# Edge loop of a graph network on one core: the running sums carried on VectorE instead of TensorE, and three copies and comparisons in another order

## The reference, cut to what matters

```python
source = x[src]; target = x[dst]
h = jax.nn.relu(concatenate([source, target, edge_attr]) @ W_msg1 + b_msg1)
aggregated = segment_sum(h @ W_msg2 + b_msg2, dst)        # layer 0
agg = segment_sum(x[src] + edge_attr_16 @ ew.T + eb, dst)  # layer 1
```

## Time and profile before

| | us |
|---|---|
| median of 3 runs | 4364.23 (4362.29 to 4392.64) |
| the profiled execution | 4381.03 |
| its span | 4379.2 |
| first gather to last store of the edge loop | about 130 to 1586 |
| GpSimd busy in that stretch | 1169.59 |
| TensorE busy in that stretch | 1163.95 |
| VectorE busy in that stretch | 1051.99 |
| ScalarE busy in that stretch | 580.05 |

### The profile page before, as it was taken

One profiled execution on the slowest core, in us unless ns is written; L12 is line 12 of the kernel. 1 busy time (PEld: TensorE's weight loads), 2 busy tenths in 40 slices (PEclk: granted clock), 3 DMA queues, 4 the chain that ended last, 5 costly groups with the idle time before them and its releaser, 6 DMA issues. The chain is left out here.

```text
span 4379.2 us, 63336 instructions
## 1 busy us (share of the span) xinstructions
PE 2767.2 (63%) x16020; PEld 1843.3 (42%) x16021; DVE 2936.8 (67%) x6155; ACT 1734.3 (40%) x3786; POOL 2009.4 (46%) x1741
## 2 busy tenths in 40 slices
PE   2687788788888866999997790782333433433442
PEld 1344454445444433777775680671211211211211
DVE  3676677677777735222249897897887857766765
ACT  4343343344444324211111460466645645544221
POOL 0687788778888851000000002000365656655565
PEclk6798898888998876999999895896666656655665
DMA  5322222222222221000000000021110111101111
GB/s 126 83 75 71 71 73 72 71 71 76 74 79 75 72 71 28 1 1 1 1 10 19 28 7 17 21 30 24 23 15 12 30 13 29 14 12 14 14 13 12
DMA packets 212371, 169.34 MB, mean 39 GB/s; under 512 B 109109, under 2 KB 189894, under 8 KB 211708
## 3 DMA queue, kind: packets, MB, share of 16 engines
q1 hardware_dynamic: 145702, 89.86, 7.8%
q0 software_dynamic: 50688, 65.00, 7.3%
q10 hardware_dynamic: 15830, 12.65, 1.1%
HBM read 143.30 MB, written 24.08 MB: 38 GB/s over the span
## 5 line engine op out<-in xcount | busy, mean ns | idle before, releaser
L503 POOL DMA_INDIRECT B_pg<-P_rows,src x784 | 1169.6, 1492 | 397.6 <-issue 216.6
L1760 POOL DMA_INDIRECT F_got<-head_rows,F_index x800 | 765.8, 957 | 915.3 <-DVE F_index L1904 632.7
L1777 PE MATMUL F_psK<-counts_T,ident 125*125 125x447 f16 (+1 forms) x700 | 364.8, 521 | 852.9 <-issue 426.7
L1777 PEld LDWEIGHTS F_psK<-counts_T,ident 125*125 125x125 f16 x700 | 131.6, 188 | 1038.6 <-issue 592.9
L1901 DVE MAX8 F_top<-F_key 125x8 f32<-125x3125 f32 x100 | 341.1, 3411 | 307.1 <-ACT F_key L1803 273.7
L1803 ACT COPY F_key<-F_psK 125x447 f32<-125x447 f32 (+1 forms) x700 | 322.1, 550 | 426.7 <-DMA C_h<-h_rows 251.8
L551 DVE TENSOR_TENSOR B_msg<-B_psE,B_pg 128x512 f32<-128x512 f32 x320 | 219.7, 686 | 346.9 <-POOLq L509 103.4
L649 PE MATMUL B_psG<-B_msg,B_hot_d 128*25 128x145 f32 x2560 | 419.1, 311 | 51.7 <-ACT B_sums L579 46.4
L634 PE MATMUL B_psC<-B_hot_m,B_hot_lo 128*128 128x325 f16 (+1 forms) x2560 | 446.2, 322 | 1.6 <-DVE B_hot_d L543 1.5
L1363 POOL PARTITION_ALL_REDUCE E_one<-E_one x1 | 0.4, 377 | 964.2 <-issue 964.2
L541 DVE TENSOR_SCALAR B_hot_m<-iota_key,B_rel 128x626 f16<-128x626 f16 x1280 | 403.5, 378 | 0.3 <-issue 0.3
(11 more groups left out here) (329 smaller groups left out, 4679.8 us busy)
## 6 DMA issues: line engine op xcount, KB each, us to landing
B_place<-edge_targets SPq DMA_DIRECT2D x80, 300.0 KB
F_got<-head_rows,F_index POOLq DMA_INDIRECT x800
B_pg<-P_rows,src POOLq DMA_INDIRECT x784
B_attr<-in_edge_attr SPq DMA_DIRECT2D x80, 128.0 KB
B_hT<-feature_parts SPq DMA_DIRECT2D x320, 27.0 KB
F_row<-a_j SPq DMA_DIRECT2D x4, 1562.5 KB
B_qw<-Q_parts SPq DMA_DIRECT2D x240, 25.0 KB
E_row<-target_bounds SPq DMA_DIRECT2D x10, 546.9 KB
```

Source lines behind the costliest of these rows:

```text
L503: nc.gpsimd.indirect_dma_start(out=pg[:, c % RING, q, :], out_offset=None, in_=t["P"], in_offset=bass.IndirectOffsetOnAxis(ap=keep["src"][ ...
L1760: nc.gpsimd.indirect_dma_start(out=got[G % 2][:, (T % GT) * TOP + i, :], out_offset=None, in_=t["tab"], in_offset=bass.IndirectOffsetOnAxi ...
L1777: nc.tensor.matmul(psK[:, q, 0:w], keep["ident16"], CT[:, u * N + c:u * N + c + w], start=True, stop=False)
```

## The change

The carried sum leaves TensorE. `sum_up` keeps its four products and drops the one with the identity. VectorE gets a new instruction per step, `add_sums`, which computes the new running sum from the old one times 1 or 0 plus `psG`; it is done for the step three back (`LAG = 3`), ahead of the step's add. ScalarE drops the copy with the factor (`prev`) and copies `run` into `sums` three steps behind instead of one. On ScalarE the two copies of the counts move ahead of the relu. On VectorE, `hot_lo` now waits until TensorE has carried the counts of two steps before (`c_ps`), and the attribute copy moves from ahead of `hot_lo` to behind `hot_d`.

```diff
+        LAG = 3
-        prev, sums = two("prev", [WD, MW], F32), two("sums", [WD, V, MW], F32)
+        run, sums = two("run", [WD, MW], F32), two("sums", [WD, V, MW], F32)
...
                 v.tensor_scalar(hT[f][0:KQ, :], place[j][:, bass.ds(at * CE, CE)], keep["base"][0:KQ, bass.ds(k, 1)], keep["rowmod"][0:KQ, :], ALU.subtract, ALU.is_equal).then_inc(hT_ready, 1)
-                v.tensor_copy(msg[f][:, :, 1:AW], attr[j][:, bass.ds(at, 1), :, :].squeeze(1)).then_inc(attr_used, 1)
+                dve.wait_ge(c_ps, k * 2 + 2)
                 v.tensor_tensor(hot_lo[b][:], keep["iota_lo"].unsqueeze(1).broadcast_to([EP, ET, EP]),
...
                                 rel[b][:, ET:2 * ET].unsqueeze(2).broadcast_to([EP, ET, WD]), ALU.is_equal).then_inc(hot_ready, 1)
+                v.tensor_copy(msg[f][:, :, 1:AW], attr[j][:, bass.ds(at, 1), :, :].squeeze(1)).then_inc(attr_used, 1)
...
+            def add_sums(k, u):
+                b = u % 2
+                dve.wait_ge(g_ps, k + 5)
+                dve.wait_ge(g_out, k + 1)
+                dve.wait_ge(run_ready, k + 2)
+                v.scalar_tensor_tensor(out=run[b][:], in0=run[1 - b][:], scalar=keep["same"][0:WD, bass.ds(k, 1)], in1=psG[b][:, 0:MW], op0=ALU.mult, op1=ALU.add).then_inc(run_ready, 1)
...
+                if not (isinstance(k, int) and k < LAG):
+                    add_sums(k - LAG, (u - LAG) % U)
...
-                act.wait_ge(g_ps, k + 5)
-                nc.scalar.activation(prev[b][:], psG[b][:, 0:MW], ACT.Copy, scale=keep["same"][0:WD, bass.ds(k + 1, 1)])
-                nc.scalar.copy(sums[j][:, bass.ds(at, 1), :].squeeze(1), psG[b][:, 0:MW]).then_inc(g_out, 1)
+                act.wait_ge(run_ready, k + 3)
+                act.wait_ge(g_out, k + 2)
+                nc.scalar.copy(sums[j][:, bass.ds(at, 1), :].squeeze(1), run[b][:]).then_inc(g_out, 1)
...
-                act.wait_ge(pre_ready, k + 3)
-                nc.scalar.activation(msg[f][:, :, 17:MW], msg[f][:, :, 17:MW], ACT.Relu).then_inc(relu_done, 1)
-                if u:
-                    take_sums(k - 1, u - 1, i, chunks[u - 1], chunks[(u - 1) // V * V])
...
                 for s in range(2):
                     act.wait_ge(c_ps, k * 2 + s + 5)
                     s0, n = s * HALF[0], HALF[s]
                     nc.scalar.copy(CT[:, s0:s0 + n, bass.ds(w * WD, WD)], psC[b][s][:, 0:n * WD].rearrange("p (s d) -> p s d", d=WD)).then_inc(c_out, 1)
+                act.wait_ge(pre_ready, k + 3)
+                nc.scalar.activation(msg[f][:, :, 17:MW], msg[f][:, :, 17:MW], ACT.Relu).then_inc(relu_done, 1)
+                if u >= LAG:
+                    take_sums(k - LAG, u - LAG, i, chunks[u - LAG], chunks[(u - LAG) // V * V])
...
                 pe.wait_ge(relu_done, k + 1)
-                pe.wait_ge(g_out, k + 1)
+                pe.wait_ge(run_ready, k + 1)
                 for q in range(ET):
-                    nc.tensor.matmul(psG[b][:, 0:MW], hot_d[f][:, q, :], msg[f][:, q, :], start=q == 0, stop=False)
-                nc.tensor.matmul(psG[b][:, 0:MW], keep["ident32"][0:WD, 0:WD], prev[1 - b][:], start=False, stop=True).then_inc(g_ps, 1)
+                    last = nc.tensor.matmul(psG[b][:, 0:MW], hot_d[f][:, q, :], msg[f][:, q, :], start=q == 0, stop=q == ET - 1)
+                last.then_inc(g_ps, 1)
```

More of the change, by code:

```diff
@@ L445, in edge_loop @@
         landed = keep["landed"]
-        (fixed, primed, rel_ready, hT_ready, hot_ready, q_ps, c_ps, g_ps, pre_ready, relu_done, c_out, g_out, p_ready, attr_used, go) = (sem(n) for n in (
-            "fixed", "primed", "rel_ready", "hT_ready", "hot_ready", "q_ps", "c_ps", "g_ps", "pre_ready", "relu_done", "c_out", "g_out", "p_ready", "attr_used", "go"))
+        (fixed, primed, rel_ready, hT_ready, hot_ready, q_ps, c_ps, g_ps, pre_ready, relu_done, c_out, g_out, p_ready, attr_used, go, run_ready) = (sem(n) for n in (
+            "fixed", "primed", "rel_ready", "hT_ready", "hot_ready", "q_ps", "c_ps", "g_ps", "pre_ready", "relu_done", "c_out", "g_out", "p_ready", "attr_used", "go", "run_ready"))
         row_v = t["row"].rearrange("(o e) -> o e", o=1)
@@ L517, in _ @@
             dve.sem_inc(attr_used, 2 * V)
+            dve.sem_inc(run_ready, 2)
             for u in range(2):
-                v.memset(prev[u][:], 0.0)
                 v.memset(sums[u][:], 0.0)
+            v.memset(run[1][:], 0.0)
             for u in range(V):
@@ L563, in _ @@
             steps(dve, body)
+            for k in range(STEPS - LAG, STEPS):
+                add_sums(k, k % U)
         @block.scalar
         def _(act):
-            act.sem_inc(g_out, 1)
+            act.sem_inc(g_out, 2)
             act.sem_inc(c_out, 4)
@@ L576, in take_sums @@
                 at = 0 if f == 0 else ahead(f + c0, c)
-                act.wait_ge(g_ps, k + 5)
-                nc.scalar.activation(prev[b][:], psG[b][:, 0:MW], ACT.Copy, scale=keep["same"][0:WD, bass.ds(k + 1, 1)])
-                nc.scalar.copy(sums[j][:, bass.ds(at, 1), :].squeeze(1), psG[b][:, 0:MW]).then_inc(g_out, 1)
+                act.wait_ge(run_ready, k + 3)
+                act.wait_ge(g_out, k + 2)
+                nc.scalar.copy(sums[j][:, bass.ds(at, 1), :].squeeze(1), run[b][:]).then_inc(g_out, 1)
                 if f == V - 1:
-                    act.wait_ge(g_out, k + 2)
+                    act.wait_ge(g_out, k + 3)
                     act.wait_ge(sums_stored[1 - j], i * 16 + 16 + 16 * j)
@@ L589, in body @@
                 w = window(k, c)
-                act.wait_ge(pre_ready, k + 3)
-                nc.scalar.activation(msg[f][:, :, 17:MW], msg[f][:, :, 17:MW], ACT.Relu).then_inc(relu_done, 1)
-                if u:
-                    take_sums(k - 1, u - 1, i, chunks[u - 1], chunks[(u - 1) // V * V])
-                elif not (isinstance(k, int) and k == 0):
-                    take_sums(k - 1, U - 1, i - 1, chunk(act, k - 1), chunk(act, k - V))
                 for s in range(2):
@@ L599, in body @@
                     nc.scalar.copy(CT[:, s0:s0 + n, bass.ds(w * WD, WD)], psC[b][s][:, 0:n * WD].rearrange("p (s d) -> p s d", d=WD)).then_inc(c_out, 1)
+                act.wait_ge(pre_ready, k + 3)
+                nc.scalar.activation(msg[f][:, :, 17:MW], msg[f][:, :, 17:MW], ACT.Relu).then_inc(relu_done, 1)
+                if u >= LAG:
+                    take_sums(k - LAG, u - LAG, i, chunks[u - LAG], chunks[(u - LAG) // V * V])
+                elif not (isinstance(k, int) and k < LAG):
+                    done = u - LAG + U
+                    take_sums(k - LAG, done, i - 1, chunk(act, k - LAG), chunk(act, k - LAG - done % V))
             steps(act, body)
-            take_sums(STEPS - 1, U - 1, STEPS // U - 1, chunks[U - 1], chunks[V])
+            for u in range(U - LAG, U):
+                take_sums(STEPS - U + u, u, STEPS // U - 1, chunks[u], chunks[V])
             for u in range(2):
```

## The result

The changed kernel took **4584.41 us** (median of 4 runs, 4557.79 to 4596.55) against 4363.41 for the kernel before: ratio **1.0481**, interval 1.0413 to 1.055. The forecast was 4314 us with a range of 4269 to 4405. It was wrong in sign and outside the range.

A forecast was written before the change was run, and what follows sets the result against it. GpSimd's gathers, held up by VectorE's comparison bursts, were taken to bound the edge loop. Terms -43 - 31 + 14 + 10 = -50 us, on the median of 4364.23, gave 4314 us, range 4269 to 4405.

The forecast's parts named there:

- the new wait of `hot_lo`: VectorE's low comparison waits for carried counts: some 25 short gaps charged 0.4 us each, +10 us.
- If `hot_lo` waits for the carry in more than 50 steps, I misjudged TensorE: Sign against the forecast at VectorE's low comparison; before, in 48 of 317 steps the carry ended after that comparison started.
- The border is missed: Rival: 94 short gaps end at about 1.5 us, gathers held, 2.1 us lost; +40 us, 4404 us, chance 0.18.
- -43 - 31 + 14: New VectorE sum lengthening gaps between comparison bursts: 94 short gaps gain 43 us, 44 middle gain 31, 58 longer cost 14.
- a border at 0.19: In the edge loop, gathers starting up to 0.14 us behind hT's start pass; hT starts 0.33 ahead of hot_lo.
- the single gather of 912.19: Gather 0.25 us ahead of hot_lo, passing in 0.96; taken to show the border goes with hT's end.
- E: End of VectorE's burst of hot_lo and four hot_m; the next gather was taken to start 1.30 us later.
- The gathers set the pace of the loop: GpSimd's gathers bound the edge loop: 980 us fixed, 426 held up, 38 waits, 1444 us in all.
- The sum's spacing of 0.28: VectorE's new running sum adds 0.24 to 0.29 us to each gap between bursts; 0.28 taken.
- The count copies ahead of the relu: ScalarE's reordering priced at 0: the relu's reader on TensorE stands a whole step further on.
- The price of dropping `prev` and the identity product: Work of 119.8 us off ScalarE and 150.1 us off TensorE, neither on GpSimd's path: priced at 0.
- The moved copy that makes VectorE the bound: Rival: attribute copy behind hot_d waits for a gather's end, 110 us more, 4475 us, chance 0.05.

The follow-up runs named there:

- fourth series: Chip 4, against the kernel before (4345.6 us): hot_lo wait alone 1.0465; copy and target comparison in quarters 1.0105; sums between low and middle comparisons 1.0256, with wait 1.034.

## Why the prediction was wrong

Two terms of the sum failed, the wait's and the new sum's. How the recorded loss of 221 us divides between them isn't known, since the changed kernel without its wait never ran where signals are late.

**The first failed step is the new wait of `hot_lo`**, "Behind this wait stand only VectorE's own preparations. It lengthens a gap where a longer gap is nearly free", priced at +10 us. What showed it wrong is the wait on chip 4: +197 us on 4346 alone, +42 with the sums inside the burst. I priced it from when the carry's rows end, and never asked when its signal reaches a waiting engine. The trace of before had the answer, in a row that I had shown: `prev` on ScalarE waits 233.4 us for "remote", on TensorE's same kind of signal, and VectorE's add has 95.6. I took ScalarE's as harmless; the loop of before follows the gathers' sum, so it had not cost much there. The change put `hot_lo` behind it, and with it the burst, the next add, and the ring. "If `hot_lo` waits for the carry in more than 50 steps, I misjudged TensorE": it does in 84, 46 of them released by "remote" and 38 by the carry's own end.

**The price depends on the chip, or on its state at the time.** Where no signal is late the wait is worth -103 us (4147.6 us for the changed kernel with the relu first, 4250.86 with both edits undone, that is with the wait gone as well) or -200 (alone, 3949.86 against 4150.13). The recorded pair's traces and the fourth series' show late signals, the three other chips' don't. The recorded trace of before has them, so a forecast had to count with them; one that let every wait on TensorE be late could have had the sign.

**The second failed step is the new sum's own term: "The border is missed" was true, and I gave it 0.18.** The forecast had -43 - 31 + 14 for the sums. With the moved copy and no wait they cost +101 us on chip 11 (1.0269), alone +114 on chip 15 (1.0283). Two pairs of GpSimd and VectorE from the version with both edits undone show why:

```profile
626.67 0.94 POOL L504 DMA_INDIRECT B_pg<-P_rows,src  x1 [0.30 <-DVE B_msg L553]
...
626.92 0.68 DVE L538 TENSOR_TENSOR B_hot_lo<-iota_key,lo 128x512 f16<-128x512 f16 x1
```

```profile
644.06 3.10 POOL L504 DMA_INDIRECT B_pg<-P_rows,src  x1 [0.30 <-issue]
...
644.28 0.67 DVE L538 TENSOR_TENSOR B_hot_lo<-iota_key,lo 128x512 f16<-128x512 f16 x1
```

A gather 0.25 ahead of `hot_lo` passes in 0.94 us, one 0.22 ahead takes 3.10. In that trace all 24 that start 0.24 to 0.32 ahead pass, and all 124 from 0.21 to 0.23 are held. I had reckoned with 0.23 ahead and a border at 0.19. The border did move with `hT` (with the copy at its old place, in the sums alone, 0.28 ahead is held and the nearest that pass start 0.35 ahead), but it stands at 0.235, further ahead of `hot_lo` than I took it on the strength of the single gather of 912.19. And the first gather behind the burst starts at E + 1.33 there and not + 1.30. **A margin of 0.01 to 0.02 us** decides 3.10 against 0.94 in 124 steps. The rival's figure for such a gather, 2.1 us lost, is close to the measured 3.10 - 0.94 = 2.16. In the trace of the sums alone 138 of 319 gaps stand at 1.30 to 1.59 us (mean 1.53), with 2.11 us lost in each; in before on the same chip 142 stood under 1.30 (mean 1.25), with 1.30. The other gaps lose 1.31 each in both, so 138 x 0.81 = 112 us accounts for the measured 114. The sign is in the recorded pair too: gathers of 2.95 us or more, of which the rival was to bring more, rise from 43 to 80. Placing the sums inside the burst instead (1.0256) doesn't help: there the gap is 1.25 again, but a held gather stays for a burst that is 0.27 us longer (2.12 against 1.85). The copy's place changes next to nothing: 1.0269 with it moved, 1.0283 without.

**What held.** "The gathers set the pace of the loop": on three chips exactly, in all versions, but not in the changed kernel where signals are late. The sum's spacing of 0.28: 910.82 to 911.10 in the changed kernel. The count copies ahead of the relu: 0 on chip 5 (1.0007), untried with late signals. The price of dropping `prev` and the identity product, 0, wasn't tested by itself, but nothing is missing in the sums' account on chip 15 without it. The moved copy that makes VectorE the bound didn't come. In the recorded trace the held-up time fell to 784 x (1.342 - 0.944) = 312 us from 426, more than forecast, but for another reason: while VectorE waits for a signal there is no burst to hold a gather. Behind gaps of over 2.2 us the gathers lose 0.42 us a burst there, and 1.26 in before.

**The rest of the recorded time.** The kernel before has a span of 4379.2 us in the recorded trace and 4142.9 on chip 15. Of the 236, 49 lie in the loop (1446 and 1397 us from first to last gather) and 187 in the last stage, whose gathers span 1251 us in the recorded trace,

```profile
L1760 POOL DMA_INDIRECT F_got<-head_rows,F_index x800: 942/947/2013, 3112.4 to 4363.7; - x160
```

against 1064. The changed kernel has 1252 and 1067, in the rows shown above, so that part is equal for both kernels and drops out of the comparison. Why the last stage takes longer there isn't known; none of its rows is released by "remote".

**What stays open.** Why signals are late: they go with gathers in full run. In the trace of before I laid each release of `prev` on ScalarE beside GpSimd's state when TensorE's product ended: with a gather running unhindered 35 of 76 came over 1 us late, with one held up 6 of 109, between two gathers 9 of 46. That is an association, and it may run the other way: while VectorE waits for a late signal, nothing holds the gathers up. Unhindered gathers alone don't do it, for on chip 15 the same kernel has no late signal. No run removed the gathers on a chip with late ones. Nor is it known whether the chip is what differs: chips 4, 5 and 11 had one series each, only chip 15 had two (and agreed with itself), so that some state at the time isn't excluded. Open too is how a wait that holds VectorE back for 16 us in all saves 200 where signals are prompt. The same instructions with a wait always met give 82 (on chip 5; the 200 are chip 11's), so some 118 come with the real holding; that they come through where the bursts fall between gathers is argued, not shown. How a met wait gives anything at all is as open.

## What to carry to other kernels

A wait costs the time until its signal arrives, and this can lie far behind the end of the row that sends it (8.8 us at the place shown). Before adding a wait to the engine that paces or feeds the bound, look for waits on the same sender that are already in the trace, and see how late those are, even where they cost nothing. Where two engines hold each other up by fixed shapes that come round with a fixed period, a shift of 0.3 us has no sign that can be argued from means; if the margin to the border is less than what one observed row can fix, give both sides the same chance. And compare a change on more than one chip if its worth hangs on phases: the best version here is 0.954 of before on one and 1.0465 on another, and none tried is faster than the kernel before on both.

## What the runs showed of the hardware

- TensorE's signal reached ScalarE and VectorE 8.8 us after the end of the sending row at the place shown, in the recorded trace; chip 4's traces have the same "remote" waits, and on chips 5, 11 and 15 no trace has one. The kernel before takes 4363 and 4346 us on the former, 4141 to 4150 on the latter.
- The gather's border is sharp to about 0.01 us in the version with both edits undone: 0.24 ahead of `hot_lo` it passes, at 0.23 it is held for the whole burst. With the attribute copy in between it lies further ahead: in the sums alone 0.28 is held and 0.35 passes.
- Held gathers leave at fixed places. In the trace of before on chip 15 they end 2.8 to 2.9 us behind the start of `hot_lo` (213 of 313), 2.0 (61) or 1.5 (37), about 0.95 behind the burst's end, or behind breaks in it. Neither a float32 copy nor a sum of 0.27 us between the comparisons lets the loop gain by such a place (1.0069 on chip 5, 1.0256 on chip 4).
